# Third layer of a four-layer graph network: where the two diagonal units of each strip stand in the order of units

## What is computed

```python
h = jnp.maximum(_layernorm(x, axis=-1), 0.0)
# inside the layer, with h as its x:
deg = jnp.maximum(adj.sum(axis=1, keepdims=True), 1e-08)
w = adj / deg
log_ij = _logmap(x[:, None, :], x[None, :, :], c)   # for every pair of nodes
agg = jnp.einsum('ij,ijc->ic', w, log_ij)
transformed = agg @ weight + bias
```

## Time and profile before

| what | value |
| --- | --- |
| median of three runs | 1219.32 us (1218.47 to 1220.24) |
| the profiled execution, its time | 1219.28 us |
| its span in the trace | 1217.5 us |
| TensorE busy, share of the span | 89% |
| VectorE, ScalarE, GpSimd busy | 70%, 62%, 32% |
| the third layer's units, from the first `sides2` to the last gather | 627 to 1062.5 us |

### The profile page before, as it was taken

The page is one execution under the profiler, slowest core; times in us unless marked ns, Lnnn a source line. Parts: engine busy times, 40 slices in busy tenths (PEclk is TensorE's granted clock), DMA queues, the critical chain, the costliest instruction groups (busy, mean ns, idle before and its releaser), DMA issues.

```text
span 1217.5 us, 15886 instructions
## 1 busy us (share of the span) xinstructions
PE 1081.6 (89%) x5064; PEld 503.5 (41%) x5084; DVE 851.6 (70%) x916; ACT 760.8 (62%) x780; POOL 393.4 (32%) x279
## 2 busy tenths in 40 slices
PE   2799999997699999999159999999999999954997
PEld 0233333336523333333124554555545454443555
DVE  7799989976756666666836767667677777666553
ACT  2355555552556666665258778778787888635864
POOL 6434423420101111110163334333343434323533
PEclk9799999997789999999569999999999999966999
DMA  9799999960068888885304545535454545211652
GB/s 325 263 351 358 350 341 339 359 250 9 1 196 287 280 281 286 288 281 180 128 0 140 171 133 179 173 124 187 139 173 138 181 131 157 67 54 44 205 184 86
DMA packets 96286, 237.97 MB, mean 195 GB/s; under 512 B 16369, under 2 KB 45041, under 8 KB 79857
## 3 DMA queue, kind: packets, MB, share of 16 engines
q1 hardware_dynamic: 87024, 220.62, 54.7%
q10 hardware_dynamic: 9216, 16.78, 3.6%
HBM read 219.55 MB, written 17.83 MB: 195 GB/s over the span
## 4 chain that ended last, share of the span: by engine, by line
PE 82%; DVE 8%; POOL 3%; issue 3%; ACT 2%; DMA 1%; SPq 0%; DVEq 0%; POOLq 0%; ACTq 0%
PE PS L452 55%; PE PS L649 10%; PE PS L595 5%; PE PS L596 4%; PE PS L672 4%; PE PS L484 1%; PE PS L462 1%; PE PS L474 1%; DVE st L1024 1%; DVE work L1021 1%; PE PS L696 1%; POOL work L408 1%; ACT work L766 1%; POOL X L401 1%; POOL brow L375 1%
## 5 line engine op out<-in xcount | busy, mean ns | idle before, releaser
L1161 DVE TENSOR_TENSOR work<-work,ring 128x1024 f32<-128x1024 f32 x128 | 151.2, 1222 | 88.6 <-ACT work L858 88.6
L415 POOL TENSOR_TENSOR ring<-work,ring 128x1024 f32<-128x1024 f32 x58 | 137.2, 2365 | 214.5 <-DVE work L1248 214.5
L801 ACT ACTIVATE work<-PS 128x1024 uint8<-128x1024 f32 x128 | 124.1, 1021 | 130.4 <-PE PS L452 130.4
L858 ACT ACTIVATE work<-PS,att_sc 128x1024 f32<-128x1024 f32 x128 | 147.4, 1201 | 88.7 <-PE PS L596 45.3
L452 PE MATMUL PS<-work,ystage 128*64 128x512 f32 x768 | 186.3, 606 | 0.1
L452 PE MATMUL PS<-ring,work 128*65 128x256 f32 (+1 forms) x568 | 183.2, 469 | 2.6 <-DVE work L1275 2.6
L1242 DVE SCALAR_TENSOR_TENSOR work<-PS,work 128x1024 f32<-128x1024 f32 x72 | 88.2, 1225 | 120.8 <-PE PS L452 107.6
L649 PE MATMUL PS<-TB,TA 65*128 65x512 f32 x288 | 139.8, 609 | 4.7 <-DVE work L1242 2.9
L381 POOL COPY ystage<-H 128x64 f32 x60 | 83.2, 1387 | 137.2 <-PE PS L452 136.9
L452 PEld LDWEIGHTS PS<-ring,work 128*65 128x65 f32 x568 | 77.2, 138 | 84.7 <-issue 62.8
L897 ACT ACTIVATE work<-work 128x1024 f32<-128x1024 f32 x72 | 76.0, 1055 | 46.1 <-DVE work L1242 45.9
(11 more groups left out here) (203 smaller groups left out, 1637.8 us busy)
## 6 DMA issues: line engine op xcount, KB each, us to landing
ring<-in_adj_t SPq DMA_DIRECT2D x96, 1024.0 KB, 5.2
ring<-in_adj_t SPq DMA_DIRECT2D x100, 512.0 KB, 3.8
work<-in_adj_t SPq DMA_DIRECT2D x32, 1024.0 KB, 7.7
codes<-work ACTq DMA_DIRECT2D x64, 256.0 KB, 6.5
ring<-codes SPq DMA_DIRECT2D x64, 256.0 KB, 3.1
H<-in_adj_t SPq DMA_DIRECT2D x28, 512.0 KB, 4.6
X<-in_x SPq DMA_DIRECT2D x2, 512.0 KB, 5.2
out_x<-X SPq DMA_DIRECT2D x2, 512.0 KB, 4.1
```

Source lines behind the costliest of these rows:

```text
L415: nc.gpsimd.tensor_tensor(near(n), sum_[:, n % ROTS, :], near(n), ALU.mult).then_inc(sem("near_ready"), 1)
L801: nc.scalar.activation(made[:, k, u * UNIT:(u + 1) * UNIT], PS[:, (4 + 2 * u) * BANK:(6 + 2 * u) * BANK], ACT.Relu).then_inc(sem("codes_ma ...
L858: nc.scalar.activation(att[:, u % 2, :], PS[:, b * BANK:(b + 2) * BANK], ACT.Sigmoid, bias=att_sc[:, 2:3], scale=att_sc[:, 1:2]).then_inc( ...
L1161: V.tensor_tensor(prob[:, u, :], att[:, u % 2, :], ring[:, s, (u % 2) * UNIT:(u % 2 + 1) * UNIT], ALU.mult)\
```

## The change

The two D units of each strip no longer stand side by side at its head. With R for a unit with a mirror image, the order within a strip goes from D D R R R R ... to R D R R D R ..., and each strip's order of R units among themselves stays. Strip 6, with four units, goes from D D R R to R D R D; strip 7 has only its two D units. So the list ends R D R D D D in place of D D R R D D. No instruction is added or removed, and all engines and the DMA queue follow the same new list.

```diff
-UNITS = [(S, p) for S in range(NS) for p in range(2 * S, T // 2)]
+def strip_order(S):
+
+    own, rest = [2 * S, 2 * S + 1], list(range(2 * S + 2, T // 2))
+    return rest[:1] + own[:1] + rest[1:3] + own[1:] + rest[3:]
+
+
+UNITS = [(S, p) for S in range(NS) for p in strip_order(S)]
```

## The result

| | before | changed |
| --- | --- | --- |
| median, 20 runs each | 1219.13 us (1217.54 to 1224.83) | 1222.30 us (1219.83 to 1224.12) |
| ratio changed / before | | 1.0021, 95% interval 1.0011 to 1.0031 |
| profiled execution, its span | 1219.28 us, 1217.5 us | 1224.00 us, 1222.3 us |

The change makes the kernel slower by about 0.2%: 2.6 us by the ratio and by the means (1222.13 against 1219.53), 3.2 us by the medians. The forecast was 1220.1 us, 0.8 above before; the range reached to 1222.6. The profiled execution of the changed kernel is among its slowest, so its 4.7 us more than the profile of before are not all the change's.

What follows compares the result with a forecast made beforehand. The prediction took TensorE to bound the kernel, with 82% of the chain. From 1219.28 us: heads - 1.25, first units - 0.9, end + 1.26, clock + 1.7, giving 1220.1 us, range 1217.4 to 1222.6.

Steps and rivals of the forecast that it cites:

- TensorE bounds the stage, and D units side by side empty it by 0.25 us: Third layer's stage: two D units side by side cost TensorE 0.25 us of standstill per strip of 14 units.
- The term for five heads, 1.25: Heads of strips 1 to 5: D units apart remove 0.25 us of standstill each, 1.25 us gained.
- The rival that the heads give nothing: Strip heads: D units apart cost as much as together, the 1.25 us is lost, 1221.4 us; chance 0.10.
- The first units, 0.9: Stage's start: unit 0's `mirror2` fills the 1.39 us wait ahead of `scores2(3)`, 0.9 us gained, bounds 0.6 and 1.0.
- The end, 1.26: End of the list: `nodes2` starts 1.26 us later without the clock's share, bounds 1.0 to 1.6.
- The 5.17, the 4.85 and the saved `far2_out`: End of the list: last `sum2` spacings of 5.17 and 4.85 us, and 0.51 us saved on VectorE.
- The clock in the wait, 1.7: TensorE's clock falls in the 4.3 us wait ahead of the last two near gathers, costing 1.7 us, between 0 and 3.44.
- The rival that the clock stays up: Wait ahead of the last two near gathers: the clock does not fall, time 1218.4 us; chance 0.24.
- The sum without the clock, 1218.4: Forecast time from heads, first units and end, without the 1.7 us for the clock's fall: 1218.4 us.
- The upper end, 1222.6: Top of the forecast range: both last near gathers and a part of `nodes2` at half clock, 1222.6 us.
- the rival of a sooner rise at the start: Third layer's first units: TensorE's clock rises sooner, worth 1.2 to 3.7 us, times 1217.2 down to 1214.7; chance 0.08.
- the slower rival: End: the clock falls in the wait and is not back before `nodes2`, which also runs slow, 1227.1 us; chance 0.12.

Runs made afterwards that it cites:

- e1: Kernel before with D units apart in strips 1 to 5 alone; median 1220.58 us of 12 runs, ratio 0.9999 to before.
- e3: Kernel before with D units apart in strips 0 to 5, strip 6 as before; median 1218.67 us of 11 runs, ratio 0.9999 to before.
- e2: Kernel before with D units apart in strip 6 alone; median 1224.73 us of 5 runs, ratio 1.0042 to before.
- e11: Changed kernel with unread matmuls in three waits: last two near gathers and the fourth layer's first step and second half; median 1217.72 us, ratio 0.9985 to before.
- e9: Kernel before with unread matmuls in three waits: last two near gathers and the fourth layer's first step and second half; median 1217.49 us, ratio 0.9977 to before.
- e5: Changed kernel run once more, its order not altered, for a second profile; median 1221.37 us of 12 runs, ratio 1.0019 to before.
- e6: Kernel before with three unread matmuls ahead of the last two near gathers; median 1219.09 us of 12 runs, ratio 0.9995 to before.
- e7: Kernel before with D units apart in strips 0 to 5 and three unread matmuls ahead of the last two near gathers; median 1219.03 us, ratio 1.0000 to before.
- e10: Kernel before with D units apart in strips 0 to 5 and unread matmuls in three waits; median 1215.40 us of 8 runs, ratio 0.9961 to before.

## Why the prediction was right in part, point by point

*TensorE bounds the stage, and D units side by side empty it by 0.25 us.* Right: 85.39 in place of 85.63 us. The term for five heads, 1.25, measured 1.07 (e1). The rival that the heads give nothing has fallen.

*The first units, 0.9.* Right: e3 less e1 gives 1.99 - 1.07 = 0.92, and the 1.39 us wait is gone.

*The end, 1.26.* Right: 1.25 (e2). The 5.17, the 4.85 and the saved `far2_out` were each as worked out.

Together these terms give 0.89 us gained at the last gathers. Measured between like executions it is 0.84 in L (e11 against e9) and 0.89 in E (mean of changed and e5 against e6).

*The clock in the wait, 1.7.* The fall came, in both profiles, and filling the wait takes it away. For the gathers alone it costs 1.70 to 2.38 us. Where it came was right only in one of them: within the wait in the first (granted 0.64 in the us from 1055), 1.3 us into the gathers in the second. The prediction had allowed for that. The rule of the Trainium skill, "TensorE: Matmul & The Clock Gate", section "HAM oscillation — how this bites in real kernels", forecast the fall, and the first profile agrees with it. The second, and the falls at waits of 2.56 and 2.55 us (e1, e3) where 2.61 us had none, show that the gap alone does not say whether and when. The rival that the clock stays up has fallen.

*What was too small* is this term as the whole price of the end, because the price was taken at these gathers alone, and all that follows `nodes2` was put at nothing. The sum without the clock, 1218.4, needs 3.9 us to reach the median of the first set and 3.0 for the second, in place of 1.7 (by the ratios 3.5 and 3.2). Some 2 us of it are the gathers. In the first profile three more places stand behind them. VectorE's addition, lengthened to 2.85 us from 1.22 as in e11, puts the first transposes behind `nodes2` 2.08 us farther from its end. The fourth layer's halves are 1.54 and 1.58 us longer, by where the clock happens to be: the same chain pieces take 48.1 or 49.7 and 31.3 or 33.0 us in other executions. The second profile has neither (addition 1.22, halves 48.11 and 31.29) but `nodes2` at 10.88 us in place of 8.79. The filled kernels support this: of 2.6 us between the two orders 0.25, with 0.9 either way, is left when three waits are filled, and in that pair's profiles the addition accounts for 1.6 us against the changed order.

That the measured 1222.30 us lies inside the range is in part luck. The upper end, 1222.6, was meant for both gathers and a part of `nodes2` at half clock. In the profile `nodes2` was shorter than before, and the time went elsewhere.

I also forecast the sum against a single profiled execution as if the part behind the stage were a constant. It is not: e1, e3 and e7 gain 1.1 to 2.0 us at the gathers, and their times do not show it.

*What stays open.* Why the changed order meets the long pieces of the fourth layer so often is not settled. A time above 1222.8 us came in 12 of its 32 runs and in 6 of the 109 of before over all sets (one of 1257.31 us left out). Whether the fall at the end moves the later ones is not shown by any run. The ruler shows that executions come in two groups already at the third layer's first units, so where the clock changes is not evenly spread over executions. With that the rival of a sooner rise at the start is open in part. The rise came 2.7 us sooner in both profiles of the changed kernel (E), but also in e6, whose order is the old one, and not in e3, e7 and e11, whose first units are the new ones. Six of nine profiles with the new start are E, and one of five with the old; these are too few to tell. Of the slower rival, clock low through `nodes2` as well, one profile (e5) shows a part: the clock was back for the beginning of `nodes2` and fell again 2.8 us into it, and it took 10.88 us in place of 8.79. Its full price of 1227.1 us was never the median.

## What to carry to other kernels

An order that removes small standstills in a long stage should be checked at its end first: what is taken from the beginning of a list is put somewhere, and three units in a row that ScalarE and VectorE bound cost here, at the end, 1.25 us plus a fall of TensorE's clock, which is more than the heads and the first units gained (1.07 and 0.92 us). The quickest version here (e10) keeps the new order away from the last strips and gives TensorE unread matmuls in three waits of 2 to 5 us: 0.9961 (0.9947 to 0.9974), by 0.4% faster than the kernel before and so than both.

A gain of one or two us can vanish behind the stage that made it, in where the clock falls and rises and in which of two engines' instructions begins first. An earlier arrival should be followed as far as the next wait of the engine that bounds. Two orders are better compared with the waits filled, from a landmark inside the trace, than by their times.

## What the runs showed that was not expected

VectorE's addition of 1.22 us takes 2.80 to 2.86 us when GpSimd's product on other data began ahead of it (six of fourteen profiles), and it then stands on the path of TensorE. The eight others have it at 1.22 or 1.23.

The fourth layer's first half took 48.1 or 49.7 us without filling and 46.81 us in each of five profiles with five unread matmuls ahead of it. That wait of 5 us costs 1.3 to 2.9 us by the clock, in the order of before too (48.12, and 49.59 in e6).

Dense work does not by itself keep the clock up. In every one of the profiles it fell within `nodes2`, whose 64 matmuls stream 65 columns each, with TensorE busy throughout (the earlier trace rows before). And the length of a wait does not decide alone either: 2.61 us left the clock full in one execution, 2.55 us did not in another.
